# A residual chain with adapter feed-forward in three-pass products: where the adapters' small products stand among the large ones

## The chip, the cores and the metric

One NeuronCore of a Trainium2 chip runs one program. The metric is device microseconds of one launch. Three runs of the kernel before gave a median of 1245.07 us (1245.03 to 1245.76).

The engines are named as the profile names them: PE (TensorE, with PEld for its weight loads), DVE (VectorE), ACT (ScalarE), POOL (GpSimd) and SP (SyncE, which only issues transfers here).

## The reference, cut to what matters

Each of the 64 samples carries a 64 x 512 array `x`. Three small layers with weights gathered by sample come first, then a feed-forward layer with low-rank adapters, and each is added to `x`:

```python
x = x + einsum('bct,bcd->bdt', x, w0[subject])
x = x + einsum('bct,bcd->bdt', x, w1[adapter])
x = x + einsum('bct,bcd->bdt', x, w2[adapter]) + bias[adapter][:, :, None]

def lora_linear(x, W, A, B, idx):         # A: (8, in, 16), B: (8, 16, out)
    base = einsum('bsd,df->bsf', x, W)
    lora = einsum('bsr,brf->bsf', einsum('bsd,bdr->bsr', x, A[idx]), B[idx])
    return base + lora

gate = lora_linear(x, Wg, Ag, Bg, idx)    # 512 -> 2048
up = lora_linear(x, Wu, Au, Bu, idx)
x = x + lora_linear(silu(gate) * up, Wd, Ad, Bd, idx)   # 2048 -> 512
```

## The kernel before, in words

The samples are done in four quarters of 16 samples, each quarter as two token tiles t = 0 and 1 of 512 columns. The hidden dimension of 2048 is done in 16 blocks of 128; a unit b = -1 ahead of them, in quarters 1 to 3, makes the rank-16 inputs of the adapters. Every large product is made of three passes in fp32r (high by high, high by low part, low by high), so an operand needs a high part, made by an ACT copy, and a low part, made by a subtraction on DVE or POOL.

Gate and up of both token tiles are four products by a scheme of Strassen's kind with seven products (`A11, S1, S2, A12, S3, S4, A22`), each six matmuls of 512 columns (`product`, recorded at L1692). They stand in the PE's program in this order, in the banks px, py, px, pz, px, py, px. Between them come four groups of the **adapters' output products** (`lora`, L1709), three small matmuls each of 192, 256 and 192 columns that add to the bank of a result: lora11 (pz), lora21 (py), lora22 (pz), lora12 (px).

DVE takes the results out of the banks: **c11** (L1513, reads pz after lora11), **u3** (L1518, px after S3), **c12** (L1523, py after lora21), **c22** (L1570, pz after lora22), with `silu0` on ACT behind c11. Then **gate0** (L1565) and **gate1** (L1575) multiply gate and up. The result h is split into a high part (ACT copy, L915) and a low part (`h_low`, POOL, L769), which the down products need.

The **down phases** take h of two blocks ("half" 0 and 1) and one token tile. At the end of an odd block stands the phase for t = 0, which needs the h of that same block in its half 1, at the end of an even block the phase for t = 1 of the two blocks before. A block 15 has both. In each half there are four large products into the banks pd0 to pd3 (three matmuls each, L1692) and one **adapters' down product** into pv: four matmuls of 256 columns (`adapters_down`, L1736 and L1738). The order of the five is `order(d)`, j = 4 being the adapters' product. DVE adds the finished banks to `acc` and `vacc` (L1475, L1472). The adapters' down product needs the tile `ad`, whose low part POOL makes (`ad_low`, L769, tile ad) in each odd block; in POOL's program it stands behind a wait for **c11** of that block. In blocks 13 and 15 of quarters 0 to 2 POOL gathers rows for the next quarter (`gather_own`, L733) between ad_low and h_low.

Each engine runs its own program in written order. Semaphores tie them: a count such as `p2_mm` (lora11 done) or `c11_done` is raised by one instruction and waited for by others. In blocks 3 to 10 of quarters 0 to 2 the PE also makes the layers of the next quarter: a product at L1998 behind S2 and a fp32 product at L2031 behind S3 ("layer blocks"), with DVE and ACT steps of their own.

Of the kernel before, what the change touches and what calls it, by code (L numbers as in the profile page):

```python
# [11 lines left out]
ACT = mybir.ActivationFunctionType  # L12
# [78 lines left out]
def cond_resid_kernel(nc, x, subject, adapter, w0_rows, w1_pairs, w2_rows, bias_pairs, w_gu, w_dn, a_in_rows, ad_rows, b_rows, bd_rows, out):  # L91
# [6 lines left out]
    with ExitStack() as ctx:  # L98
# [216 lines left out]
        p6_mm = sem("p6_mm")  # L315
        p2_mm = sem("p2_mm")
        p7_mm = sem("p7_mm")
        p3_mm = sem("p3_mm")
# [48 lines left out]
        def made(q, i):  # L367

            return q * QP + i + 1

        def order(d):

            return (4, 0, 1, 2, 3) if stays(d) else (0, 1, 4, 2, 3)

# [159 lines left out]
        def _(sp):  # L534
# [104 lines left out]
            for q, b in units():  # L639
# [56 lines left out]
                if b == BLOCKS - 1 and q + 1 < QUARTERS:  # L696
                    for half in range(2):
                        sp.wait_ge(xops_out[half], TP * (q + 1) * 64)

                    for done, k in ((p1_mm, A11), (p5_mm, S1), (p2_mm, A12), (p4_mm, A22), (p6_mm, S2), (p7_mm, S3),  # L700
                                    (p3_mm, S4)):
                        sp.wait_ge(done, k_done)
                        for g, xo in enumerate((xo_hi, xo_lo)):
                            sp.dma_start(raw(xo[:, k, :]), xops[g, k]).then_inc(xop_in[k], 16)
                    load_down(blocks_done(q, b))
                    load_down(blocks_done(q, b) + 1)
                elif k is None and n and n + 2 < QUARTERS * UNITS:
                    next_weights(n)
# [204 lines left out]
        def _(act):  # L913
# [122 lines left out]
            for q, b in units():  # L1036
# [97 lines left out]
                if b != 1 and n > 1:  # L1134
                    act.wait_ge(p2_mm, k)
                    if split:
                        weights_high(n + 1, 1)
                act.wait_ge(c11_done, k)
                act.activation(g0[:, :], g0[:, :], ACT.Silu).then_inc(silu0_done, 1)
                if (q, b) == (0, BLOCKS - 1):  # L1140
                    own_selectors(1).then_inc(sel_done, 1)
                if n == 1:
                    weights_high(n + 1, 0)
                i = pair_at(q, b)
                if i is not None:
                    pair = PAIR_ORDER[i]
                    act.wait_ge(layer_mm, made(q, i))
                    add_bias(acc[:, (q + 1) % 2, pair, :], pd[0][:, :], (q + 1) * QP + pair).then_inc(layer_add, 1)

                def keep_c21():  # L1150
# [18 lines left out]
                if b == 1:  # L1169
                    act.wait_ge(p2_mm, k)  # L1170
                    weights_high(n + 1, 0)
                    weights_high(n + 1, 1)
# [34 lines left out]
        def _(dve):  # L1207
# [346 lines left out]
            for q, b in units():  # L1554
# [30 lines left out]
                if b == 0:  # L1585
                    if q:
                        v_low(q - 1, 1)
                        sums(n + 1)
                    c11(k)
                    if q:  # L1590
                        weights_low(n + 1, 0)
                    u3(k)
                    select(q, 1)
                    c12(k)
                    if not q:
# [42 lines left out]
                if to_own:  # L1638
                    own_difference(q + 1)
                c11(k)  # L1640

                behind = parts_at(q, b) is not None
# [6 lines left out]
                if behind:  # L1649
                    weights_low(n + 1, 1)  # L1650
                    token_low(q, parts_at(q, b))
                c12(k)
                gate0()
                if late:
                    sums(n + 1)
                    weights_low(n + 1, 0)
# [31 lines left out]
        def _(pe):  # L1688
# [97 lines left out]
            def down(q, m, t, layer=0, turned=0, finished=0):  # L1786

                d = phase(q, m, t)
                for half in range(2):
                    pe.wait_ge(h_lo_done[t], q * BLOCKS + 2 * m + half + 1)  # L1790
                    pe.wait_ge(dn_done, q * BLOCKS + 2 * m + half + 1)
                    for r, j in enumerate(order(d)):
                        if half == 0 and d:
# [8 lines left out]
                        if j == 4:  # L1802
                            if half == 0:
                                pe.wait_ge(ad_done, q * SUPER + m + 1)
                            ins = adapters_down(t, half)
                        else:
                            ins = split_product(pd[j][:, :], [s[:, j * P:(j + 1) * P] for s in hs],
# [139 lines left out]
            for q, b in units():  # L1947
# [6 lines left out]
                if b == -1:  # L1954
                    pe.wait_ge(c21_kept, k)
                    own_products(q, 1)
                    finish(q - 1, 0)
                    pe.wait_ge(c22_done, k)
                    select(q, 0)
                    continue  # L1960
# [46 lines left out]
                if fresh:  # L2007
                    tokens_ready(q, A12)
                product(pz, A12, True, True)

# [4 lines left out]

                if n > 1:
                    lora11()

                pe.wait_ge(w_done[2], n + 1)
# [3 lines left out]
                product(px, S3, False, True).then_inc(p7_mm, 1)  # L2023
                if n == 1:

                    lora11()
                if i is not None:
# [13 lines left out]
                if fresh:  # L2041
                    tokens_ready(q, S4)
                product(py, S4, False, True)
                lora(py, b, 1, 0).then_inc(p3_mm, 1)

# [5 lines left out]

                if b:
                    lora22()

                pe.wait_ge(w_done[3], n + 1)
# [3 lines left out]
                product(px, A22, False, True)  # L2059
                if b == 0:  # L2060
                    pe.wait_ge(b_got_in[1], (q * SUPER + 1) * CHUNKS * 16)
                    pe.wait_ge(u_done, 6 * q + 6)
# [98 lines left out]
```

## Time and profile before

| | before |
|---|---|
| median of 3 runs | 1245.07 us |
| span of the profiled execution | 1244.1 us |
| PE busy | 1235.7 us, 99% |
| PEld busy | 1036.6 us, 83% |
| DVE busy | 954.8 us, 77% |
| POOL busy | 713.4 us, 57% |
| ACT busy | 551.6 us, 44% |
| granted PE clock | 0.999 |

The page gives the span of the profiled execution, not a launch time of its own for it, so the span stands for it. A busy PE isn't a PE at its peak, since matmuls are pipelined: what a matmul costs is the distance from its start to the start of the next, which the timeline gives. A timeline row with x3 holds three instructions that touch, from the first one's start.

### The profile page before, as it was taken

What the parts mean: (1) busy time and instruction counts of PE and PEld (TensorE: products, weight loads), DVE (VectorE), ACT (ScalarE), POOL (GpSimd) and SP (SyncE); (2) the same over time, 40 slices, a digit from 0 to 9 for tenths busy, and PEclk for the clock granted to TensorE, in tenths of its full rate; (3) what the DMA queues carried; (4) which work ended last, traced back from release to release, by engine and by line L of the source; (5) the groups of instructions that cost most, each with busy time, mean ns of one, the idle gap of its engine ahead of it and who ended that gap; (6) DMA issues with size and microseconds to landing.
All of it is one profiled execution on the core that took longest, in us unless ns stands there. A gap on an engine that the chain in (4) does not pass through costs nothing.

```text
span 1244.1 us, 17944 instructions
## 1 busy us (share of the span) xinstructions
PE 1235.7 (99%) x6222; PEld 1036.6 (83%) x6222; DVE 954.8 (77%) x1531; ACT 551.6 (44%) x987; POOL 713.4 (57%) x598
## 2 busy tenths in 40 slices
PE   8999999999999999999999999999999999999998
PEld 7888888888888888888888888888888888888887
DVE  6987778887778777788778768777868877777775
ACT  3744454444434354554334444544534443444332
POOL 3576556558745556546865556564675554444553
PEclk9999999999999999999999999999999999999999
DMA  5866455544896345456398534545559742333433
GB/s 195 271 227 209 118 143 150 155 137 136 304 330 216 106 126 150 128 141 176 109 383 294 168 108 145 153 126 148 147 177 374 254 114 78 97 85 102 111 90 121
DMA packets 142199, 211.68 MB, mean 170 GB/s; under 512 B 44192, under 2 KB 88480, under 8 KB 142112
## 3 DMA queue, kind: packets, MB, share of 16 engines
q1 hardware_dynamic: 117696, 135.45, 34.5%
q0 software_dynamic: 23552, 73.95, 19.6%
q8 instruction: 51, 0.84, 0.3%
q10 hardware_dynamic: 864, 1.15, 0.3%
q14 instruction: 36, 0.29, 0.1%
HBM read 166.46 MB, written 44.04 MB: 169 GB/s over the span
## 4 chain that ended last, share of the span: by engine, by line
PE 96%; DVE 2%; DMA 0%; issue 0%; another core or an unknown queue 0%; DVEq 0%
PE px L1692 28%; PE pd L1692 28%; PE py L1692 14%; PE pz L1692 7%; PE pz L1709 3%; PE pv L1738 2%; PE pv L1736 2%; PE pd L2031 2%; PE py L1709 2%; PE px L1709 2%; PE pd L1861 1%; PE pd L1719 1%; PE py L1843 1%; PE px L1843 1%; PE pd L1828 1%; PE pd L1901 0%
## 5 line engine op out<-in xcount | busy, mean ns | idle before, releaser
L769 POOL TENSOR_TENSOR h_lo<-g,h_hi 128x512 fp32r<-128x512 f32 x127 | 182.9, 1440 | 283.6 <-ACT h_hi L915 281.3
L733 POOL DMA_INDIRECT b_got<-b_table,idx_b x192 | 199.4, 1039 | 58.0 <-issue 51.1
L1692 PE MATMUL px<-xo_hi,wg_hi 128*128 128x512 f32 x516 | 206.9, 401 | 1.1 <-DVE wg_lo L1345 0.8
L1475 DVE TENSOR_TENSOR acc<-pd,acc 128x512 f32<-128x512 f32 x248 | 164.7, 685 | 53.8 <-PE pd L1692 51.3
L1345 DVE TENSOR_TENSOR wg_lo<-w_raw,wg_hi 128x512 fp32r<-128x512 f32 (+1 forms) x256 | 182.3, 717 | 29.9 <-issue 17.9
L1692 PE MATMUL px<-xo_hi,wg_lo 128*128 128x512 f32 x516 | 202.4, 392 | 0.0
L1692 PE MATMUL px<-xo_lo,wg_hi 128*128 128x512 f32 x516 | 200.9, 389 | 0.0
L915 ACT ACTIVATE wg_hi<-w_raw 128x512 fp32r<-128x512 f32 (+1 forms) x260 | 146.0, 570 | 122.8 <-PE py L1709 77.0
L1692 PE MATMUL pd<-wd_hi,h_hi 128*128 128x512 f32 x504 | 199.7, 396 | 0.0
L1692 PE MATMUL pd<-wd_lo,h_hi 128*128 128x512 f32 x504 | 197.9, 393 | 0.0
L1692 PE MATMUL pd<-wd_hi,h_lo 128*128 128x512 f32 x504 | 196.6, 390 | 0.0
L915 ACT ACTIVATE h_hi<-g 128x512 fp32r<-128x512 f32 x128 | 80.9, 632 | 194.5 <-DVE g L1565 75.4
L1692 PEld LDWEIGHTS px<-xo_hi,wg_lo 128*128 128x128 f32 x516 | 96.8, 188 | 22.1
L1692 PEld LDWEIGHTS pd<-wd_hi,h_lo 128*128 128x128 f32 x504 | 94.6, 188 | 21.7
L1692 PE MATMUL py<-xo_hi,wg_hi 128*128 128x512 f32 x260 | 111.6, 429 | 0.0
L1692 PEld LDWEIGHTS px<-xo_hi,wg_hi 128*128 128x128 f32 x516 | 96.9, 188 | 17.4 <-DVE wg_lo L1345 1.0
L1692 PEld LDWEIGHTS px<-xo_lo,wg_hi 128*128 128x128 f32 x516 | 97.5, 189 | 15.6
L1692 PEld LDWEIGHTS pd<-wd_hi,h_hi 128*128 128x128 f32 x504 | 94.5, 188 | 13.9
L1692 PEld LDWEIGHTS pd<-wd_lo,h_hi 128*128 128x128 f32 x504 | 94.8, 188 | 12.9
L915 ACT ACTIVATE g<-px 128x512 f32<-128x512 f32 x64 | 38.4, 600 | 149.5 <-PE px L1692 138.9
L1575 DVE TENSOR_TENSOR g<-g,up 128x512 f32<-128x512 f32 x64 | 100.6, 1572 | 3.5 <-ACT g L1154 2.7
L1692 PE MATMUL py<-xo_hi,wg_lo 128*128 128x512 f32 x260 | 101.8, 391 | 0.0
(325 smaller groups left out, 2454.0 us busy)
## 6 DMA issues: line engine op xcount, KB each, us to landing
w_raw<-w_gu SPq DMA_DIRECT2D x65, 512.0 KB
wd_raw<-w_dn SPq DMA_DIRECT2D x64, 256.0 KB
xo_hi<-xops SPq DMA_DIRECT2D x21, 512.0 KB, 6.0
xo_lo<-xops SPq DMA_DIRECT2D x21, 512.0 KB, 7.3
acc<-x SPq DMA_DIRECT2D x8, 1024.0 KB, 8.7
ad_raw<-ad_table SPq DMA_DIRECT2D x16, 512.0 KB
xops<-st_hi SPq DMA_DIRECT2D x24, 256.0 KB, 2.7
xops<-st_lo SPq DMA_DIRECT2D x24, 256.0 KB, 2.9
```

The source lines that it names most:

```text
L733: gp.indirect_dma_start(out=dst, out_offset=None, in_=rows_of, in_offset=bass.IndirectOffsetOnAxis(ap=rows.bitcast(U32), axis=0)).then_inc ...
L769: return gp.tensor_tensor(dst, src_raw, src_hi, ALU.subtract)
L915: return act.activation(dst, src, ACT.Copy)
L1345: dve.tensor_tensor(wg_lo[:, lo:hi, :], src, wg_hi[:, lo:hi, :], ALU.subtract).then_inc(w_done[g], 1)
L1475: ins = dve.tensor_tensor(dst, pd[j][:, :], dst, ALU.add)
L1575: dve.tensor_tensor(g1[:, :], g1[:, :], up1[:, :], ALU.mult).then_inc(h_done[1], 1)
L1692: ins = pe.matmul(psum, w_parts[wi], x_parts[xi], start=(start and i == 0), stop=(stop and i == 2), skip_group_check=more)
L1709: ins = pe.matmul(psum[:, tokens], b_got[:, CHUNKS * t + c, first:first + P], u[:, m, t, cols], start=(start and c == 0), stop=True, skip_ ...
L1736: pe.matmul(pv[:, tok], ad[:, half, 2 * t + a, :, :].rearrange("p g n -> p (g n)"), hs[0][:, tok], start=(half == 0 and a == 0), stop=True ...
L1738: ins = pe.matmul(pv[0:HC, tok], ad[:, half, 2 * t + a, 0, :], hs[1][:, tok], start=False, stop=True, skip_group_check=True)
L1843: ins = pe.matmul(ua_bank(q, t, 0)[:, a * HALF:(a + 1) * HALF], w_parts[wi][:, cols], (xo_hi, xo_lo)[xi][:, k, tok], start=(cp == c == a = ...
L2031: pe.matmul(pd[0][:, :], f_one[:, :], acc[:, (q + 1) % 2, PAIR_ORDER[i], :], start=True, stop=True).then_inc(layer_mm, 1)
```

## The change

Four things move, and the number of instructions with work in them stays the same.

1. lora11 moves from behind A12 to behind S4, right ahead of lora21. A new count `a12_mm` tells the end of A12 to those who waited for it by `p2_mm`.
2. lora22 moves from behind lora21 to behind A22, right ahead of lora12 (blocks 1 to 15).
3. In the phases for t = 0, and in the last one of a quarter's t = 1, the adapters' down product is the first of half 0 and the last of half 1. In the other phases for t = 1 (`early`) the adapters' products of both halves are the first two of the phase. The last two phases of the program stay as they are.
4. DVE's and ACT's programs follow: c11 goes behind the low part of the weights and u3, silu0 behind it, `token_low` behind gate0.

```diff
+        def early(d):
+
+            return d % 2 == 1 and d % (2 * SUPER) != 2 * SUPER - 1
+
         def order(d):
 
-            return (4, 0, 1, 2, 3) if stays(d) else (0, 1, 4, 2, 3)
+            return (4, 0, 1, 2, 3) if stays(d) or early(d) else (0, 1, 2, 3, 4)
...
-                product(pz, A12, True, True)
+                product(pz, A12, True, True).then_inc(a12_mm, 1)
...
-                if n > 1:
-                    lora11()
...
                 product(py, S4, False, True)
+                lora11()
                 lora(py, b, 1, 0).then_inc(p3_mm, 1)
...
-                if b:
-                    lora22()
...
                 product(px, A22, False, True)
-                if b == 0:
+                if b:
+                    lora22()
+                else:
...
-                    for r, j in enumerate(order(d)):
+                    for r, j in enumerate(order(d) if half else (4, 0, 1, 2, 3)):
+                        if half and j == 4 and early(d):
+                            continue
...
                             ins = adapters_down(t, half)
+                            if half == 0 and early(d):
+                                pe.wait_ge(h_lo_done[t], q * BLOCKS + 2 * m + 2)
+                                adapters_down(t, 1).then_inc(down_mm, 1)
...
-                c11(k)
-
                 behind = parts_at(q, b) is not None
                 if not last and not behind and not late and not to_own:
                     weights_low(n + 1, 1)
...
                 if behind:
                     weights_low(n + 1, 1)
-                    token_low(q, parts_at(q, b))
+                c11(k)
                 c12(k)
                 gate0()
+                if behind:
+                    token_low(q, parts_at(q, b))
```

The last two pieces of the diff are DVE's, in blocks 1 to 15. In block 15 of quarters 0 to 2 the four weight sums of the next unit (`sums(n + 2)`) stand behind u3 as before, and so now ahead of c11. A wait for the last add into pv is new ahead of `select(q, 0)` in the unit b = -1. POOL's program isn't changed.

On the PE, in quarter 3 before: lora11 (pz<-u,b_got) between A12 (pz) and S3 (px).

```order
L1692 MATMUL pz<-xo_hi,wg_lo 128x512
L1709 MATMUL pz<-u,b_got 128x192
L1709 MATMUL pz<-u,b_got 128x256
L1709 MATMUL pz<-u,b_got 128x192
L1692 MATMUL px<-xo_hi,wg_hi 128x512
L1692 MATMUL px<-xo_lo,wg_hi 128x512
```

After, in the same quarter: behind S4 (py), with lora21, ahead of A22 (px).

```order
L1697 MATMUL py<-xo_hi,wg_lo 128x512
L1714 MATMUL pz<-u,b_got 128x192
L1714 MATMUL pz<-u,b_got 128x256
L1714 MATMUL pz<-u,b_got 128x192
L1714 MATMUL py<-u,b_got 128x192
L1714 MATMUL py<-u,b_got 128x256
L1714 MATMUL py<-u,b_got 128x192
L1697 MATMUL px<-xo_hi,wg_hi 128x512
```

Nothing small stands between A12 and the end of S4 any more; there are two places with six small matmuls a block in place of one with six and two with three.

The PE at the start of a phase of quarter 3 before, from the last matmul of lora12 (px<-u) on: pd0, pd1, then the adapters' product (pv<-h,ad).

```order
L1709 MATMUL px<-u,b_got 128x192
L1692 MATMUL pd0<-wd_hi,h_hi 128x512
L1692 MATMUL pd0<-wd_lo,h_hi 128x512
L1692 MATMUL pd0<-wd_hi,h_lo 128x512
L1692 MATMUL pd1<-wd_hi,h_hi 128x512
L1692 MATMUL pd1<-wd_lo,h_hi 128x512
L1692 MATMUL pd1<-wd_hi,h_lo 128x512
L1736 MATMUL pv<-h_hi,ad 128x256
L1738 MATMUL pv<-h_lo,ad 64x256
L1736 MATMUL pv<-h_hi,ad 128x256
L1738 MATMUL pv<-h_lo,ad 64x256
L1692 MATMUL pd2<-wd_hi,h_hi 128x512
```

After, the phase for t = 0: the adapters' product stands right behind lora12.

```order
L1714 MATMUL px<-u,b_got 128x192
L1741 MATMUL pv<-h_hi,ad 128x256
L1743 MATMUL pv<-h_lo,ad 64x256
L1741 MATMUL pv<-h_hi,ad 128x256
L1743 MATMUL pv<-h_lo,ad 64x256
L1697 MATMUL pd0<-wd_hi,h_hi 128x512
L1697 MATMUL pd0<-wd_lo,h_hi 128x512
L1697 MATMUL pd0<-wd_hi,h_lo 128x512
```

It needs `ad` six large matmuls earlier than before, and the other adapters' product of this phase has gone to its end.

DVE in a block of quarter 3 before: c11 is g0<-pz,g0, u3 is up1<-px,up1, c12 is up0<-py,up0, gate0 is g0<-g0,up0.

```order
L1345 TENSOR_TENSOR wg_lo<-w_raw,wg_hi 128x512
L1513 TENSOR_TENSOR g0<-pz,g0 128x512
L1345 TENSOR_TENSOR wg_lo<-w_raw,wg_hi 128x512
L1518 TENSOR_TENSOR up1<-px,up1 128x512
L1523 TENSOR_TENSOR up0<-py,up0 128x512
L1565 TENSOR_TENSOR g0<-g0,up0 128x512
L1570 TENSOR_TENSOR up1<-pz,up1 128x512
L1345 TENSOR_TENSOR wg_lo<-w_raw,wg_hi 128x512
L1575 TENSOR_TENSOR g1<-g1,up1 128x512
```

After, the same steps.

```order
L1350 TENSOR_TENSOR wg_lo<-w_raw,wg_hi 128x512 x2
L1523 TENSOR_TENSOR up1<-px,up1 128x512
L1518 TENSOR_TENSOR g0<-pz,g0 128x512
L1528 TENSOR_TENSOR up0<-py,up0 128x512
L1570 TENSOR_TENSOR g0<-g0,up0 128x512
L1575 TENSOR_TENSOR up1<-pz,up1 128x512
L1350 TENSOR_TENSOR wg_lo<-w_raw,wg_hi 128x512
L1580 TENSOR_TENSOR g1<-g1,up1 128x512
```

c11 now stands directly ahead of c12 and gate0.

## Rows read from the trace of the kernel before

**Rows 1.** The page, part 4: shares of the chain that ended last, by engine

```profile
PE 96%; DVE 2%; DMA 0%; issue 0%; another core or an unknown queue 0%; DVEq 0%
```

**Rows 2.** Timeline, PE, blocks 8 and 9 of quarter 3: start us, us, engine, line, operation

```profile
1099.67 0.48 PE L1709 MATMUL py<-u,b_got 128*128 128x192 f32 x3
1099.99 0.50 PE L1709 MATMUL pz<-u,b_got 128*128 128x192 f32 x3
1100.33 0.41 PE L1692 MATMUL px<-xo_hi,wg_hi 128*128 128x512 f32 x1
...
1101.74 0.48 PE L1709 MATMUL px<-u,b_got 128*128 128x192 f32 x3
...
1103.47 0.28 PE L1736 MATMUL pv<-h_hi,ad 128*128 128x256 f32 x1
...
1103.93 0.40 PE L1692 MATMUL pd<-wd_hi,h_hi 128*128 128x512 f32 x1
...
1107.14 0.40 PE L1692 MATMUL pd<-wd_hi,h_hi 128*128 128x512 f32 x1
...
1109.90 0.39 PE L1692 MATMUL py<-xo_hi,wg_hi 128*128 128x512 f32 x1
...
1113.98 0.48 PE L1709 MATMUL pz<-u,b_got 128*128 128x192 f32 x3
...
1117.09 0.48 PE L1709 MATMUL py<-u,b_got 128*128 128x192 f32 x3
```

**Rows 3.** Timeline, PE and PEld, the last block of the program

```profile
1221.57 0.48 PE L1709 MATMUL py<-u,b_got 128*128 128x192 f32 x3
...
1223.86 0.19 PEld L1736 LDWEIGHTS pv<-h_hi,ad 128*128 128x128 f32 x1
1223.95 0.30 PE L1736 MATMUL pv<-h_hi,ad 128*128 128x256 f32 x1
...
1224.44 0.40 PE L1692 MATMUL pd<-wd_hi,h_hi 128*128 128x512 f32 x1
...
1227.18 0.28 PE L1736 MATMUL pv<-h_hi,ad 128*128 128x256 f32 x1
```

**Rows 4.** Timeline, DVE and POOL, block 9 of quarter 3

```profile
1114.50 0.69 DVE L1513 TENSOR_TENSOR g<-pz,g 128x512 f32<-128x512 f32 x1 [1.14 <-PE pz L1709]
1115.27 1.74 POOL L769 TENSOR_TENSOR ad<-ad_raw,ad 128x512 fp32r<-128x512 f32 x1 [4.37 <-DVE g L1513]
...
1118.40 0.69 DVE L1565 TENSOR_TENSOR g<-g,up 128x512 f32<-128x512 f32 x1
...
1119.84 1.61 POOL L769 TENSOR_TENSOR h_lo<-g,h_hi 128x512 fp32r<-128x512 f32 x1 [2.83 <-ACT h_hi L915]
1120.30 1.69 DVE L1575 TENSOR_TENSOR g<-g,up 128x512 f32<-128x512 f32 x1
```

**Rows 5.** Tile ad on POOL (ns min/median/max), then timeline of block 1, quarter 1

```profile
L769 POOL TENSOR_TENSOR ad<-ad_raw,ad x32: 1278/1716/1746, 67.4 to 1219.8; 128x512 fp32r<-128x512 f32 x32
369.36 1.31 POOL L769 TENSOR_TENSOR ad<-ad_raw,ad 128x512 fp32r<-128x512 f32 x1
369.94 0.69 DVE L1518 TENSOR_TENSOR up<-px,up 128x512 f32<-128x512 f32 x1 [0.71 <-PE px L1692]
```

**Rows 6.** Timeline, DVE and PEld, block 2 of quarter 0

```profile
84.95 0.69 DVE L1518 TENSOR_TENSOR up<-px,up 128x512 f32<-128x512 f32 x1
...
85.76 0.19 PEld L1692 LDWEIGHTS px<-xo_hi,wg_hi 128*128 128x128 f32 x1 [0.51 <-issue]
```

**Rows 7.** Timeline, POOL, block 13 of quarter 1

```profile
592.67 0.96 POOL L733 DMA_INDIRECT st_lo<-a_in_rows,idx_own  x1
593.94 0.95 POOL L733 DMA_INDIRECT st_lo<-a_in_rows,idx_own  x1 [0.30 <-issue]
```

**Rows 8.** Timeline, DVE, block 15 of quarter 1

```profile
626.25 0.69 DVE L1518 TENSOR_TENSOR up<-px,up 128x512 f32<-128x512 f32 x1 [0.72 <-PE px L1692]
...
628.32 0.68 DVE L1523 TENSOR_TENSOR up<-py,up 128x512 f32<-128x512 f32 x1
```

More of the change, by code:

```diff
@@ L316, in cond_resid_kernel @@
         p2_mm = sem("p2_mm")
+        a12_mm = sem("a12_mm")
         p7_mm = sem("p7_mm")
@@ L698, in _ @@
                         sp.wait_ge(xops_out[half], TP * (q + 1) * 64)
-                    for done, k in ((p1_mm, A11), (p5_mm, S1), (p2_mm, A12), (p4_mm, A22), (p6_mm, S2), (p7_mm, S3),
+                    for done, k in ((p1_mm, A11), (p5_mm, S1), (a12_mm, A12), (p4_mm, A22), (p6_mm, S2), (p7_mm, S3),
                                     (p3_mm, S4)):
@@ L1134, in _ @@
                 if b != 1 and n > 1:
-                    act.wait_ge(p2_mm, k)
+                    act.wait_ge(a12_mm, k)
                     if split:
                         weights_high(n + 1, 1)
[L1138 to L1143, printed above, removed]
                 i = pair_at(q, b)
@@ L1148, in _ @@
                     add_bias(acc[:, (q + 1) % 2, pair, :], pd[0][:, :], (q + 1) * QP + pair).then_inc(layer_add, 1)
+                if (q, b) == (0, BLOCKS - 1):
+                    own_selectors(1).then_inc(sel_done, 1)
+                act.wait_ge(c11_done, k)
+                act.activation(g0[:, :], g0[:, :], ACT.Silu).then_inc(silu0_done, 1)
+                if n == 1:
+                    weights_high(n + 1, 0)
                 def keep_c21():
@@ L1169, in _ @@
                 if b == 1:
-                    act.wait_ge(p2_mm, k)
+                    act.wait_ge(a12_mm, k)
                     weights_high(n + 1, 0)
@@ L1639, in _ @@
                     own_difference(q + 1)
-                c11(k)
                 behind = parts_at(q, b) is not None
@@ L1650, in _ @@
                     weights_low(n + 1, 1)
-                    token_low(q, parts_at(q, b))
+                c11(k)
                 c12(k)
                 gate0()
+                if behind:
+                    token_low(q, parts_at(q, b))
                 if late:
@@ L1958, in _ @@
                     pe.wait_ge(c22_done, k)
+                    pe.wait_ge(down_add, added(phase(q - 1, SUPER - 1, 1), 4))
                     select(q, 0)
@@ L2023, in _ @@
                 product(px, S3, False, True).then_inc(p7_mm, 1)
-                if n == 1:
-                    lora11()
                 if i is not None:
```

## The prediction

> **What bounds the kernel now.** I read the chain of waits first: 96% of it is the PE itself, and DVE has 2% [rows 1]. So time can only come from the distances between the PE's matmuls, or go into waits of the PE that aren't there yet. Then I read the PE's timeline for distances from start to start. Eighteen large matmuls far from any small one take 1113.98 - 1109.90 = 4.08 us, 0.227 us each. The six of A22, right behind adapters' products, take 1101.74 - 1100.33 = 1.41 us, not 1.36. A group of three small ones takes 0.32 us (1099.67 to 1099.99), and 0.34 us when it follows another group (to 1100.33). So a small group costs its own time and slows what comes behind, for some ten matmuls: the twelve behind an adapters' down product take 1109.90 - 1107.14 = 2.76 us, not 2.72 [rows 2]. Last I read DVE and POOL around c11, ad_low and gate0 [rows 4, 5], since the change moves c11.
>
> **What the PE gains.** From one lora21 to the next a plain block (no layer product) takes 1117.09 - 1099.67 = 17.42 us before [rows 2]. After, from the same rows: lora11 and lora21 0.32 + 0.34; A22 1.41; lora22 and lora12 0.32 + 0.34; then the down phase. An adapters' product behind lora stands once in the trace: 1224.44 - 1223.95 = 0.49 us, and twelve large ones behind it take 2.74 us to 1227.18 [rows 3]. Elsewhere the product takes 1103.93 - 1103.47 = 0.46 us [rows 2].
> - Phase t = 0: 0.49 + 24 large ones (2.74 + 2.72) + 0.46, then twelve at 2.76 and 24 undisturbed ones at 5.44. With the 2.73 us of the groups and A22 that is 17.34 us, 0.08 less.
> - Phase t = 1, both products first: 0.49 + 0.47 + 5.46, then 36 undisturbed at 8.16: 17.31 us, 0.11 less.
>
> In the 24 layer blocks the layer product still stands before S4, and moving lora11 saves nothing: of its 0.04 to 0.05 us the second group's 0.02 and the slow matmuls behind the layer product eat all. They keep 0.03 and 0.06. Of the 28 t = 0 blocks (1 to 13) 16 are plain, and likewise of the 28 with t = 1 (2 to 14): 16 x 0.08 + 12 x 0.03 + 16 x 0.11 + 12 x 0.06 = 4.1 us. Blocks 0 and 15, worked the same way, add about 0.5. The gain is **4.6 us**. Merging two groups itself gains nothing (0.34 against 0.32); it is the undisturbed S3 and S4 and the undisturbed 24 down products that gain.
>
> **What the new places wait for.** I count from M, the end of lora21 (1221.57 + 0.48 = 1222.05 in the last block). The PE wants the weights `ad` at 1223.86, M + 1.81, when the adapters' product is right behind lora12 [rows 3]. Before, it stood six large ones (1.41 us) later, and ad_low began at c11's end three to four us before M: 1115.19 to 1115.27 [rows 4]. Now lora11 ends 0.34 before M. c11 starts 0.04 behind lora11's end (1114.46 to 1114.50), takes 0.69, and POOL starts 0.08 behind it: M + 0.47 [rows 2, 4]. How long does ad_low take there? Its median is 1.72 us, but 1.31 when only a DVE step that reads a bank runs beside it, u3 here [rows 5]. The 1.74 of block 9 has the low part of the weights, both inputs in SBUF, running at its start. In its new place it begins beside c12, which reads a bank, and gate0 comes later. I take 1.30: the end is at M + 1.77. From a releaser's end to the PE's next weight load took 85.76 - 85.64 = 0.12 us [rows 6]. So the weights come at M + 1.89, **0.07 to 0.08 us late** in 28 odd blocks: 2.1 us; bounds 0 (0.1 us of luck in the chain) and 0.5 us a block (ad_low at its median).
>
> The Trainium skill, SBUF — State Buffer, section "Who interferes with whom", says that a DVE instruction with at most one SBUF input doesn't contend with GpSimd, that one with two does, and that issue order decides who is blocked. By that rule ad_low keeps 1.30 and gate0 waits for it. The trace agrees for u3 (1.31 beside 0.69) [rows 5].
>
> **Gate0 is held.** gate1, begun under h_low, ended 1121.99 - 1121.45 = 0.54 us behind it [rows 4]. gate0 would start at M + 1.18 and end 0.54 behind ad_low, at M + 2.31, against M + 1.52 before. The h_high copy and the hand-over take 1119.84 - 1119.09 = 0.75 us [rows 4], and h_low 1.61 with the weights' low part at its start: M + 4.67, ready for a weight load at M + 4.79. The PE wants it at half 1, M + 1.90 + 0.49 + 2.74 - 0.23 = M + 4.90 [rows 3], and 0.07 later with the wait above. It is covered, with 0.2 us left.
>
> Block 13 of quarters 0 to 2 isn't. Between ad_low and h_low POOL issues two gathers, the last of which ends 594.89 - 592.53 = 2.36 us behind ad_low [rows 7]: M + 4.13. h_low takes 1.3 to 1.6 and ends at M + 5.4 to 5.7, while the PE can go without a wait up to M + 4.85. That is 0.5 to 0.8, say 0.65 us, three times: **1.9 us** (0 if the gathers shift earlier).
>
> Block 15 of quarters 0 to 2: the four sums behind u3 take 628.32 - 626.25 = 2.07 us with u3 [rows 8]. u3 starts at M - 2.01 (S4 and two groups, 2.05, ahead of M, plus 0.04), so c11 starts at M + 0.06 instead of M - 0.30, and `ad` is 0.37 later still: 0.45 us, three times, **1.4 us** (bounds 0.9 and 1.8).
>
> Unit b = -1: the last add into vacc is now the fifth, not the third, so the fold and mask behind it come later and with them the low part that the first product of block 0 waits for; I take 0.15 us, three times, 0.4 us, bounded by 0 and by two adds, 1.3 us each. The last block and the start (block 2 of quarter 0 waits for u3 today) 0.2 us. The new wait ahead of `select` is hidden by the products in front of it. The wait of lora22 for c11 is hidden by A22: c11 ends at M + 0.39, the weights are wanted at M + 1.1. The later c11 delays `silu0` and `token_low`, whose users come a block later; SP's stores and the load of ad_raw behind them move with them and have several us.
>
> **Sum.** -4.6 + 2.1 + 1.9 + 1.4 + 0.4 + 0.2 = +1.4 us. The span of the profiled execution is 1244.1 and the median 1245.07, 0.97 above; I keep that distance: 1244.1 + 1.4 + 0.97 = **1246.5 us**.
>
> **Rivals.**
> - *The waits stay away.* If ad_low or its hand-over is 0.08 us shorter than I build it, and the gathers of block 13 don't push h_low, only 0.9 to 1.5 us of waits is left: -3.4 us, 1241.7. For it: 0.07 us is within the roundings of a chain of five rows. Against it: blocks 13 and 15 don't hang on roundings. 21%.
> - *The new waits grow (slower).* One mechanism, ad_low in the odd blocks: each 0.1 us that it ends later costs 2.8 us over 28 blocks. The result turns slower from 0.03 us a block with the rest as it is, and is over 0.2% from 0.12. If it takes its median of 1.72 in the new place, the wait is 0.5 us: 12 us more, 1258; halfway, 1252. For it: 24 of 32 ad_low stand near 1.72. Against it: those have another step beside them. 22%.
> - *No gain at the seams.* The slow matmuls behind small ones might belong to what they read and stay, so that only the waits come: 1245.07 + 6.0 = 1251. Against it: the same 1.41 stands behind every lora group. 6%. The Trainium skill, TensorE: Matmul & The Clock Gate, section "Back-to-back issue gap", gives one distance for each width, whatever stands before (512 columns: 216 ns by its formula). By that rule no order of matmuls gains. The trace has 227 ns undisturbed and 235 on average in A22, so it differs.
> - *My sum*, 51%: 1243.5 to 1248.5.
>
> **How the numbers follow.** What a measurement can tell from no change is about 0.2%, 2.5 us: below 1242.6 is faster, above 1247.6 slower. Faster has the first rival, 0.20, and a sliver of my own case, 0.01. Slower has the second, the third and 0.10 of my own case: 0.38. Within it 0.41. The range leaves out the tail of the second rival and half of the first: 1241.8 to 1250.6.
>
> **What would show it.** In the new trace S3 and S4 without anything small between take 2.72 us; 24 down products stand in a row at 5.46; ad_low starts 0.47 behind lora21's end and lasts 1.30; gate0 lasts over 1.0 us in odd blocks; the first weight load of the adapters' down product starts 1.88 behind lora21's end instead of 1.81, and in blocks 13 and 15 of the first three quarters the PE stands for half a microsecond. The prediction is wrong if ad_low lasts 1.7 there, if blocks 13 have no wait, or if A22's 1.41 us turns up in S3 as well.

## The result

| | before | after |
|---|---|---|
| median | 1245.23 us (4 runs) | 1263.24 us (1258.95 to 1265.07, 4 runs) |
| span of the profiled execution | 1244.1 | 1257.1 |
| PE busy | 1235.7 | 1237.0 |
| DVE busy | 954.8 | 979.1 |
| chain that ended last: PE, DVE | 96%, 2% | 89%, 6% |

The ratio is 1.0138 (1.0127 to 1.0150): 18 us slower by the medians, where 1.4 us were forecast and the range ended at 1250.6. The profiled execution (1258.95 us) is the fastest of the four, 13.0 us longer in span than before. The median is 4.3 us above it, and the other three executions have no profile. The chain's shares answer to [rows 1]:

```profile
PE 89%; DVE 6%; issue 1%; DMA 1%; POOL 1%; ACT 1%; DVEq 0%; ACTq 0%
```

**Where the blocks are as forecast.** The PE's and POOL's timelines of block 9, quarter 3, after, answer to [rows 2, 4]; then the tile ad on POOL, as in [rows 5]:

```profile
1127.08 0.39 PE L1697 MATMUL px<-xo_hi,wg_hi 128*128 128x512 f32 x1
...
1129.80 0.48 PE L1714 MATMUL pz<-u,b_got 128*128 128x192 f32 x3
1130.12 0.50 PE L1714 MATMUL py<-u,b_got 128*128 128x192 f32 x3
...
1132.54 0.36 PE L1741 MATMUL pv<-h_hi,ad 128*128 128x256 f32 x1
...
1133.08 0.40 PE L1697 MATMUL pd<-wd_hi,h_hi 128*128 128x512 f32 x1
...
1138.54 0.28 PE L1741 MATMUL pv<-h_hi,ad 128*128 128x256 f32 x1
```
```profile
1130.32 0.69 DVE L1518 TENSOR_TENSOR g<-pz,g 128x512 f32<-128x512 f32 x1 [0.99 <-PE pz L1714]
1131.71 1.22 DVE L1570 TENSOR_TENSOR g<-g,up 128x512 f32<-128x512 f32 x1
```
```profile
1131.09 1.30 POOL L774 TENSOR_TENSOR ad<-ad_raw,ad 128x512 fp32r<-128x512 f32 x1 [7.07 <-DVE g L1518]
```
```profile
L774 POOL TENSOR_TENSOR ad<-ad_raw,ad x32: 1280/1296/1304, 65.9 to 1235.3; 128x512 fp32r<-128x512 f32 x32
```

S3 and S4, twelve large products, take 1129.80 - 1127.08 = 2.72 us, and the 24 down products 1138.54 - 1133.08 = 5.46. lora21 ends at 1130.62; this end is M, as in the prediction. ad_low starts at M + 0.47 in 29 of the 32 odd blocks (M + 0.85 in the three blocks 15 of quarters 0 to 2) and takes 1.30 in all 32; the weights for pv are taken in at M + 1.88 in the blocks 1 to 13 (2.26 in those three blocks 15); gate0 is held and takes 1.22 in place of 0.69. All of that stood in the forecast.

**Where the time is.** From the view of the PE's waits, after (engine, tile and line, what was waited for, us in all, times, longest); before, every wait in this view lies in the program's start and its first blocks:

```profile
PE pv L1741 <- DVE vacc L1477: 3.5, 3, 1.4
PE py L1853 <- DVE wg_lo L1345: 2.5, 3, 1.5
...
PE px L1697 <- ACT up L920: 1.5, 4, 0.4
PE py L1853 <- issue: 1.4, 2, 1.1
PE pd L1697 <- POOL h_lo L774: 1.2, 3, 0.4
...
PE px L1697 <- DVE up L1523: 1.0, 1, 1.0
PE pv L1741 <- POOL ad L774: 0.7, 3, 0.2
PE px L1697 <- issue: 0.5, 1, 0.5
```

L1853 is the adapters' first products of the next quarter (`own_products`), which stand between the two phases of block 15. To place the loss I took, from the PE's timeline, the distance from the end of one lora21 to the end of the next (us; the three numbers are the ends of quarters 0, 1 and 2):

| | block 15 to block 0 of the next quarter | block 13 to 14 | 14 to 15 (with a phase t = 1) | 9 to 10, quarter 3 (with a phase t = 0) |
|---|---|---|---|---|
| before | 34.21, 34.21, 34.22 | 17.41, 17.41, 17.41 | 17.41 | 17.41 |
| after | 37.15, 38.41, 38.63 | 18.82, 18.83, 18.83 | 17.33 | 17.40 |

The three quarter ends cost 2.94 + 4.20 + 4.42 = 11.6 us and the three blocks 13 cost 1.41 + 1.42 + 1.42 = 4.2. The rest is -2.8 us: -2.8 up to the first lora21 (50.8 us from the PE's first step, 53.6 before; over all profiles of this study 50.8 to 54.3, so one span alone tells nothing below some 3 us), +1.2 in the next three blocks, +0.2 at the end of the program, and -1.4 in all the others. Without the shorter start the span would have grown by 15.8 us.

**The quarter end, before.** ACT's, DVE's, POOL's and PE's timelines at the end of quarter 1, where lora21 of block 15 ends at M = 627.91:

```profile
633.01 1.14 ACT L915 ACTIVATE wg_hi<-st_lo 128x512 fp32r<-128x512 f32 x2
```
```profile
633.66 1.29 DVE L1340 TENSOR_TENSOR wg_lo<-st_lo,wg_hi 128x512 fp32r<-128x512 f32 x2 [1.22 <-ACT wg_hi L915]
```
```profile
627.06 1.05 POOL L733 DMA_INDIRECT st_lo<-a_in_rows,idx_own  x1
```
```profile
636.28 0.28 PE L1843 MATMUL py<-xo_hi,wg_hi 128*128 128x256 f32 x1
```

**And after**, where M = 631.60 (ACT, DVE, POOL, PE):

```profile
640.08 1.15 ACT L920 ACTIVATE wg_hi<-st_lo 128x512 fp32r<-128x512 f32 x2 [2.42 <-DMA st_lo<-a_in_rows,idx_own]
```
```profile
640.74 2.73 DVE L1345 TENSOR_TENSOR wg_lo<-st_lo,wg_hi 128x512 fp32r<-128x512 f32 x2 [3.75 <-issue]
643.39 2.47 DVE L1480 TENSOR_TENSOR acc<-pd,acc 128x512 f32<-128x512 f32 x4
645.79 0.67 DVE L1477 TENSOR_TENSOR vacc<-pv,vacc 128x512 f32<-128x512 f32 x1
```
```profile
632.45 1.28 POOL L774 TENSOR_TENSOR ad<-ad_raw,ad 128x512 fp32r<-128x512 f32 x1 [3.60 <-DVE g L1518]
633.88 1.24 POOL L738 DMA_INDIRECT st_lo<-a_in_rows,idx_own  x1
```
```profile
640.25 0.28 PE L1743 MATMUL pv<-h_lo,ad 128*64 128x256 f32 x1
641.58 0.35 PE L1853 MATMUL py<-xo_hi,wg_hi 128*128 128x256 f32 x1 [1.05 <-issue]
...
643.62 0.36 PE L1853 MATMUL py<-xo_hi,wg_hi 128*128 128x256 f32 x1 [0.38 <-issue]
...
646.72 0.35 PE L1741 MATMUL pv<-h_hi,ad 128*128 128x256 f32 x1 [1.44 <-DVE vacc L1477]
```

Read it from POOL down. The last gather of the next quarter's weights is behind ad_low and so behind c11. It was issued at M - 0.85 and is now issued at M + 2.28. Before, ACT's copy of it began 5.95 us behind the issue, right behind another copy; now it begins 6.20 behind the issue and waited 2.42 for the transfer. DVE's low part is late by it, and the first `own_products` start at M + 9.98, where the row of matmuls would have had them at M + 8.77 (0.12 us behind the start of 640.25). The second low part runs beside POOL's h_low and is longer, and `own_products` wait a second time (643.62). In DVE's program the five adds of the phase stand behind the low parts, the add out of pv as the last, and the next phase begins with pv: 1.44 us more. That is three waits in a row, with one late transfer at the head of them. (At the end of quarter 0 the low parts take their 1.29 us: 0.8 and 0.6 us of waits and, in block 0, the 0.5 of the last line of the waits.)

### The profile page after: what moved, and what is told of

The parts are those of the page before. It is cut to its first block, busy times and chain, and to the rows that moved or that the text cites. A ratio compares the mean times of both kernels' runs of the same rounds, so it can differ in the third digit from the quotient of the medians.

```text
span 1257.1 us, 17947 instructions
## 1 busy us (share of the span) xinstructions
PE 1237.0 (98%) x6222; PEld 1037.6 (83%) x6222; DVE 979.1 (78%) x1531; ACT 542.4 (43%) x987; POOL 709.9 (56%) x598
## 4 chain that ended last, share of the span: by engine, by line
PE 89%; DVE 6%; issue 1%; DMA 1%; POOL 1%; ACT 1%; DVEq 0%; ACTq 0%
PE px L1697 27%; PE pd L1697 25%; PE py L1697 13%; PE pz L1697 6%; PE pz L1714 3%; PE pv L1741 2%; PE pv L1743 2%; PE pd L2036 2%; PE px L1714 2%; PE py L1714 1%; PE pd L1871 1%; DMA st_lo<-a_in_rows,idx_own 1%; PE pd L1724 1%; DVE acc L1480 1%; PE px L1853 1%
## 5 line engine op out<-in xcount | busy, mean ns | idle before, releaser
L774 POOL TENSOR_TENSOR h_lo<-g,h_hi 128x512 fp32r<-128x512 f32 x127 | 180.3, 1420 | 232.9 <-ACT h_hi L920 231.7
L1350 DVE TENSOR_TENSOR wg_lo<-w_raw,wg_hi 128x512 fp32r<-128x512 f32 (+1 forms) x256 | 196.6, 775 | 74.9 <-ACT wg_hi L920 52.7
L1697 PE MATMUL pd<-wd_hi,h_hi 128*128 128x512 f32 x504 | 196.9, 391 | 1.2 <-POOL h_lo L774 1.2
L774 POOL TENSOR_TENSOR ad<-ad_raw,ad 128x512 fp32r<-128x512 f32 x32 | 41.5, 1296 | 166.5 <-DVE g L1518 166.5
L1151 ACT ACTIVATE g<-g 128x512 f32<-128x512 f32 x64 | 40.5, 632 | 173.8 <-DVE g L1518 173.8
L1580 DVE TENSOR_TENSOR g<-g,up 128x512 f32<-128x512 f32 x64 | 107.3, 1676 | 3.1 <-ACT g L1159 2.8
```

The source lines that it names most:

```text
L774: return gp.tensor_tensor(dst, src_raw, src_hi, ALU.subtract)
L1350: dve.tensor_tensor(wg_lo[:, lo:hi, :], src, wg_hi[:, lo:hi, :], ALU.subtract).then_inc(w_done[g], 1)
L1580: dve.tensor_tensor(g1[:, :], g1[:, :], up1[:, :], ALU.mult).then_inc(h_done[1], 1)
L1697: ins = pe.matmul(psum, w_parts[wi], x_parts[xi], start=(start and i == 0), stop=(stop and i == 2), skip_group_check=more)
```

## The experiments

The ratio is to runs of before on the same chip; the last two columns are the distances of the table above, from the profiled execution.

| kernel | median us | before us | ratio (95%) | quarter ends | blocks 13 to 14 |
|---|---|---|---|---|---|
| 1, gate part only | 1257.1 | 1245.6 | 1.0091 (1.0071 to 1.0110) | 39.37, 35.46, 35.37 | 18.13, 18.85, 18.10 |
| 2, down order only | 1243.03 | 1245.6 | 0.9977 (0.9965 to 0.9988) | 34.23, 34.65, 34.27 | 17.38 (all) |
| 3, after, gathers moved | 1247.29 | 1245.6 | 1.0009 (0.9999 to 1.0019) | 34.99, 34.97, 35.22 | 17.43, 17.40, 17.40 |
| 4, after, old order in block 15 | 1262.24 | 1245.6 | 1.0126 (1.0099 to 1.0153) | 37.89, 37.25, 39.58 | 18.83, 18.77, 18.77 |
| 5, as 3, ad_low early | 1246.35 | 1243.16 | 1.0026 (1.0017 to 1.0035) | 35.71, 35.75, 36.00 | 17.34 (all) |
| 6, before, POOL late | 1250.99 | 1243.16 | 1.0065 (1.0049 to 1.0080) | 34.65, 35.01, 34.98 | 17.77 (all) |
| 7, as 5, c11 ahead of sums | 1244.22 | 1243.16 | 1.0009 (1.0000 to 1.0018) | 35.11, 35.10, 35.38 | 17.34 (all) |
| 8, as 5, sums behind gate0 | 1242.69 | 1243.79 | 0.9992 (0.9983 to 1.0001) | 34.74, 34.77, 34.15 | 17.34 (all) |
| 9, as 2, again | 1241.39 | 1243.79 | 0.9983 (0.9973 to 0.9992) | 34.10 (all) | 17.38 (all) |
| 10, after, h_low of t = 1 early | 1260.35 (1 run) | 1245.66 | | 39.35, 35.82, 39.55 | 18.10, 18.15, 18.11 |

**1, the gate part alone.** The kernel after, with the down phases of before:

```diff
-            return (4, 0, 1, 2, 3) if stays(d) or early(d) else (0, 1, 2, 3, 4)
+            return (4, 0, 1, 2, 3) if stays(d) else (0, 1, 4, 2, 3)
```

> The kernel after, with the down phases as they were before: only lora11 and lora22, DVE's and ACT's order are changed. Theory T (late gather): POOL waits for c11 ahead of ad_low in every odd block, and c11 now comes three to four us later, so the two gathers of block 13 push h_low back and the gather of block 15 lands late. The loss of blocks 13 and 14 (1.4 us, three times) and the wait of the next quarter's first weights (1.4 us, three times) stay, the wait for the add into pv goes: 1250 to 1256 us, about 1253. Rival R (bank order): the loss at the quarter's end comes from pv being the last of one phase and the first of the next; then it is gone here, and only blocks 13 and 14 are left: 1246 to 1248.

It took 1257.1, a little over theory T's range and far from rival R's. The first `own_products` for quarter 1 waited longer than in the kernel after, with no add out of pv ahead of the low part (PE's timeline):

```profile
336.57 0.35 PE L1844 MATMUL py<-xo_hi,wg_hi 128*128 128x256 f32 x1 [3.47 <-DVE wg_lo L1341]
```

So the larger part of the loss, 11.5 us of 18, comes with the part of the change that moves c11. At the other two ends the copy began at M + 7.66 and M + 6.91 and 1.2 us each were lost.

**2, the order of the down products alone,** in the kernel before (the phases' pieces of the diff ahead and nothing of the gate's).

> The kernel before, with only the order of the adapters' down products changed, pv first of half 0 and last of half 1, both first in early phases. c11 and POOL stand as before. Theory T: POOL's gathers are in time, so the add into pv isn't late either; what is left is the gain of longer runs of large matmuls, some 2 us: 1242 to 1245, about 1243. Rival R: the quarter ends lose 3 us each as in the kernel after: 1251 to 1256.

1243.03, as T has it: faster than before. Each plain block takes 0.03 to 0.04 us less, and two of the three quarter ends lose nothing, with pv last in one phase and first in the next. So the order by itself is no cause while the transfer is in time. The third end, 34.65, lost 0.44: there ACT waited for the transfer though it was issued as early as before, and the first product of block 0 waits (ACT, then PE):

```profile
632.65 1.15 ACT L919 ACTIVATE wg_hi<-st_lo 128x512 fp32r<-128x512 f32 x2 [0.38 <-DMA st_lo<-a_in_rows,idx_own]
```
```profile
651.22 0.47 PE L1696 MATMUL px<-xo_hi,wg_hi 128*128 128x512 f32 x1 [0.34 <-issue]
```

A copy that starts 0.47 us later than before costs nearly all of it here: the row of DVE steps from that low part to block 0 has no room with this order.

The two parts don't add up: alone they are 11.5 us slower and 2.6 us faster, together 18.0 slower. Some 6 us of the rest are waits that only both together have in the profiles: for the add out of pv (3.5 us), and for ad, 0.06 us in 28 blocks and some 0.4 in three blocks 15. The others aren't placed.

**3, the gathers moved** in the kernel after (POOL's program):

```diff
+                if to_own and b % 2:
+                    gather_own(q + 1, range(11, 12) if b == BLOCKS - 3 else range(7, 8))
                 if b % 2:
                     gp.wait_ge(c11_done, k)
                     ad_low(q, b // 2)
...
-                if to_own:
-                    gather_own(q + 1, {-3: range(11, 13), -2: (), -1: range(7, 8)}[b - BLOCKS])
...
                     h_low(q, b, 0)
+                if to_own and b == BLOCKS - 3:
+                    gather_own(q + 1, range(12, 13))
```

> The kernel after, with three gathers of each of the first three quarters moved in POOL's program: in block 13 one of the two stands ahead of the wait for c11 and ad_low, the other behind h_low, in block 15 the one stands ahead of the wait for c11. Theory T: the losses of blocks 13 and 14 (4.2 us) and nearly all of the quarter ends (11.6 us, of which some 0.5 each stays as the wait for ad) go, and with them the spread of the runs: 1243 to 1248, about 1246. Rival R: only blocks 13 and 14 come back, 4 us: 1257 to 1260.

1247.29: 16 us of the 18 come back from the place of three instructions in each quarter, and the loss of blocks 13 to 14 is gone. That is T's, and R is out. Of the PE's waits these two lie behind the first blocks, the second being that for ad in the blocks 15:

```profile
PE px L1699 <- issue: 0.9, 3, 0.5
PE pv L1743 <- POOL ad L774: 0.7, 3, 0.2
```

**4, the old order in the two phases of block 15.**

```diff
+            if d % (2 * SUPER) >= 2 * SUPER - 2 and not stays(d):
+                return (0, 1, 4, 2, 3)
```

> The kernel after, with the two phases of block 15 of the first three quarters in the order of before (pv third in both halves). Theory T: the gather of block 15 is as late as before this edit, so the first weights of the next quarter are still waited for; only the wait for the add into pv (1.44 us in the profile) and the wait for ad (0.4 us) go, three times each: 4 to 6 us less than the kernel after, 1257 to 1260. Rival R: all of the loss at the quarter ends goes, 9 to 11 us: 1250 to 1254.

1262.24, by its ratio not told apart from the kernel after: less of a gain than T said, and nothing of R's. The wait for pv is gone, and the one for the weights is longer (the PE's and DVE's rows at the end of quarter 2):

```profile
953.84 0.36 PE L1855 MATMUL py<-xo_hi,wg_hi 128*128 128x256 f32 x1 [3.59 <-DVE wg_lo L1347]
```
```profile
951.40 2.89 DVE L1347 TENSOR_TENSOR wg_lo<-st_lo,wg_hi 128x512 fp32r<-128x512 f32 x2 [4.16 <-ACT wg_hi L922]
```
```profile
951.85 1.28 POOL L776 TENSOR_TENSOR h_lo<-g,h_hi 128x512 fp32r<-128x512 f32 x1
```

Here the transfer was 6.81 us from issue to ACT's copy. The two low parts then fall beside POOL's h_low and take 2.89 in place of 1.29 us. So with pv third in both phases its add isn't waited for, with the low parts this late. That the edit itself makes the transfer longer isn't shown: in experiments 1, 4 and 10, whose gather is issued at the same M + 2.28 to 2.30 as in the kernel after, the time from issue to copy lies between 4.60 and 7.20 us over nine quarter ends, and the ends with less than 5.4 us lose 1.2 to 1.6, the others 3 to 5.4. So one profile of such an end says little of its edit; the medians do.

**5, ad_low early** as well:

```diff
-                    gp.wait_ge(c11_done, k)
+                    gp.wait_ge(p7_mm, k)
                     ad_low(q, b // 2)
```

> The kernel after with the gathers moved as in the run on the gathers (1247.3 us), and ad_low of every odd block waiting for the end of S3 (p7_mm) instead of c11. Theory T: the adapters' down product waits 0.07 to 0.08 us for ad in the 28 odd blocks 1 to 13 and some 0.4 in three blocks 15 (with the restart of the row of matmuls 0.25 more there); all of it goes, since ad_low starts two microseconds before lora21's end: 2 to 3.5 us less, 1243.8 to 1245.3. gate0 is no longer held by ad_low: 0.69 us in place of 1.22. Rival R: the blocks with t = 0 do not get faster, because the 0.07 us is the restart behind lora and not a wait for ad; 1246.5 to 1247.5.

In the blocks T holds: the distance behind an odd block is 17.34 us, not 17.40, and gate0 is at 0.69. Each of the 28 blocks had waited 0.06 us. But the whole, 1.0026, is over T's range and no better than experiment 3's, since the three blocks 15 have a new wait (the PE's, DVE's and POOL's rows at the end of quarter 1):

```profile
632.01 0.49 PE L1716 MATMUL pz<-u,b_got 128*128 128x192 f32 x2 [1.17 <-DVE g L1520]
```
```profile
628.05 2.17 DVE L1336 TENSOR_TENSOR w_raw<-w_raw 128x256 f32<-128x256 f32 x1
630.15 0.41 DVE L1337 TENSOR_TENSOR w_raw<-w_raw 128x256 f32<-128x256 f32 x1
...
631.27 0.68 DVE L1520 TENSOR_TENSOR g<-pz,g 128x512 f32<-128x512 f32 x1
```
```profile
628.64 1.30 POOL L774 TENSOR_TENSOR ad<-ad_raw,ad 128x512 fp32r<-128x512 f32 x1
```

The first of the four weight sums takes 2.17 us, where the next takes 0.41, and ends 0.28 behind ad_low, which ran beside it; in [rows 8] all four sums and u3 take 2.07. c11 stands behind the sums and lora22 waits for it. Neither theory had this.

**6, only POOL late, in the kernel before:**

```diff
-                    gp.wait_ge(c11_done, k)
+                    gp.wait_ge(p3_mm if to_own else c11_done, k)
                     ad_low(q, b // 2)
```

> The kernel before with one edit: in blocks 13 and 15 of the first three quarters POOL's ad_low waits for lora21 (p3_mm) instead of c11, so the gathers behind it are issued some three us later; PE's, DVE's and ACT's programs are those of before. Theory T: the late gather alone brings the loss: the next quarter's first weights are 0.5 to 4 us late at each of the three quarter ends, and h_low of block 13 up to 0.5 us: 1247 to 1256, about 1250, with a spread between runs of several us. Rival R: POOL's lateness alone is covered and the loss needs the new order on DVE and PE as well: 1245 to 1246.

1250.99, 1.0065: T's. PE, DVE and ACT have their programs of before, and POOL's steps alone, with the gather issued at M + 1.79 instead of M - 0.85 (2.64 us later), cost 8 us in the median. So lateness on POOL is a cause by itself, of 8 of the 18 us. The profiled execution is the mildest of the four (span 1245.6, the others 1248.6 to 1249.7): its quarter ends lose 2.0 us and its blocks 13 1.1, and where the others lose more no profile shows. The PE's wait in it, then POOL's gather and ACT's copy at the end of quarter 1 (M = 627.53):

```profile
PE py L1843 <- DVE wg_lo L1340: 1.2, 3, 0.5
```
```profile
629.32 1.24 POOL L733 DMA_INDIRECT st_lo<-a_in_rows,idx_own  x1
```
```profile
635.10 1.15 ACT L915 ACTIVATE wg_hi<-st_lo 128x512 fp32r<-128x512 f32 x2 [1.99 <-DMA st_lo<-a_in_rows,idx_own]
```

**7 and 8, the sums of block 15.** Experiment 5 with `sums(n + 2)` between c11 and c12 (7), and behind gate0 (8):

```diff
-                if to_own:
-                    sums(n + 2)
                 if behind:
                     weights_low(n + 1, 1)
                 c11(k)
                 c12(k)
                 gate0()
+                if to_own:
+                    sums(n + 2)
```

> As the run with the gathers and ad_low moved, and in block 15 of the first three quarters c11 ahead of the four weight sums (sums) on DVE, not behind. Theory T: c11 and gate0 of block 15 come 0.4 us earlier, but with ad no longer waiting for c11 nothing on the PE waits for them, so at most 0.1 us a quarter: within 0.5 us of that run, 1243.5 to 1245.3. Rival R: the sums are wanted by the unit after (its weights), and behind c11 they come late: 1 to 3 us more than that run.

> As the run with gathers, ad_low and sums moved (1.0009 of before), with the four weight sums of block 15 behind gate0 instead of between c11 and c12. Theory T: in that run c12 ended at lora21's end + 2.53 us and h_low at + 5.42, and half 1 of the first phase waited 0.2 to 0.4 us for it at each of three quarter ends; now c12 ends at + 0.98, h_low is in time and 1.2 to 2 us go. Then all waits of the change are gone and only the gain of longer rows of large matmuls is left, less half a microsecond at the start: 0.9980 of before, range 0.9970 to 0.9995. Rival R: the sums now come late for the unit behind, which waits: 1.001 or more.

7 is at 1.0009, 8 at 0.9992 (0.9983 to 1.0001). In 7 the wait of lora22 is gone, and c12 and h_low are late instead (35.1 to 35.4 us at the ends). 7 is 2.1 us faster than 5, where T gave at most 0.1 us a quarter and R a loss: T had left out the wait of lora22 for c11. 8 takes that away too. It still loses 0.5 us at two of the three ends and 0.6 in the first blocks, and is level with before or a little better, where T hoped for 0.9980.

> The kernel with only the order of the adapters' down products changed, a second time, beside the run above on the same chip. It had 0.9977 of before (0.9965 to 0.9988) and its profile shows 0.03 to 0.04 us less in each block, 1.9 us in all. Theory T: 0.9975 to 0.9990 again. Rival R: the first ratio was luck in the spread of before's runs and it stands at 0.9995 to 1.0005.

0.9983 (0.9973 to 0.9992), beside 8 on the same chip. The version that beats both kernels is the smallest: before with the down order alone.

**10, the second wait behind block 13.** In the kernel after S3 of block 14 waits for ACT's copy of S2's bank (1.5 us in the waits above, with one of block 1). `h_low` of t = 1 in block 13 is put ahead of the last three gathers of the adapters' rows:

```diff
-                if b == BLOCKS - 1:
+                if b == BLOCKS - 1 or to_own and b == BLOCKS - 3:
                     h_low(q, b, 1)
...
-                if b < BLOCKS - 1:
+                if b < BLOCKS - 1 and not (to_own and b == BLOCKS - 3):
                     h_low(q, b, 1)
```

The two waits in the kernel after, block 13 of quarter 1 and S3 of block 14 (PE's timeline):

```profile
601.21 0.50 PE L1697 MATMUL pd<-wd_hi,h_hi 128*128 128x512 f32 x1 [0.39 <-POOL h_lo L774]
601.54 0.40 PE L1697 MATMUL pd<-wd_lo,h_hi 128*128 128x512 f32 x1
...
610.60 0.47 PE L1697 MATMUL px<-xo_hi,wg_hi 128*128 128x512 f32 x1 [0.44 <-ACT up L920]
```

> The kernel after, with POOL's h_low for t = 1 of block 13 in the first three quarters ahead of the last gathers of adapters' rows, some four us earlier than now. In the kernel after, S3 of block 14 waits 0.4 us in each of the three quarters: ACT copies S2's bank (up<-px) 1.05 us behind S2's end instead of 0.24, because the count of S2's end (p6_mm) rises 0.94 to 0.97 us behind the modelled end of its last matmul, while that h_low and DVE's low part of the weights, both begun 0.1 to 0.2 us before, run side by side. Theory T: the overlap brings it; with h_low elsewhere the stretch from block 13 to 14 takes 18.2 us in place of 18.8, and S3 of block 14 does not wait. Rival R: it has to do with the gathers' traffic or with the place in the program, and S3 of block 14 waits as before: 18.8. The whole is not told apart by one run: 1256 to 1264.

The distance went to 18.10 to 18.15 us, and S3 of block 14 did not wait in any of the three quarters. So of the 1.41 us of blocks 13 to 14, 0.70 is h_low of t = 0 behind the two gathers, and 0.71 this. That DVE's and POOL's steps side by side hold the copy isn't shown, and the record speaks against it as the whole cause: in experiment 1 the same h_low and low part run side by side in all three quarters and only the one with 18.85 has the wait, and in experiment 6 they do so in all three without it. So the cause of the 0.71 us stays open, and three quarters without the wait are a thin proof that moving h_low removed it.

## Why the prediction was wrong

- **The gain of the blocks.** Right in kind, a little large. 0.08 (t = 0) and 0.11 us (t = 1) were forecast for plain blocks; measured are 0.07 (17.41 to 17.34, without the wait for ad) and 0.08 (to 17.33). Layer blocks gained 0.02 and 0.04 for 0.03 and 0.06 (experiment 5 against before). Over the 56 blocks 1 to 14 that is 3.2 us for 4.1.
- **The wait for ad in 28 blocks.** Right: 0.06 us (17.40 against 17.34), ad_low at 1.30 from M + 0.47, gate0 held.
- **Block 13.** The mechanism was right, the size not: 0.65 us forecast, 1.41 measured. h_low is 0.4 late, as worked out, and the row of matmuls restarts at a longer distance (0.33 us from the first to the second); the other half is the wait of S3 in block 14, which no term of the sum has.
- **Block 15 and unit b = -1.** This is the step that failed. The prediction says that `ad` is 0.37 later there (right: 0.38), and prices block 15 at 0.45 us and the unit at 0.15, 1.8 us for the three ends; measured are 11.6. It followed POOL's gathers behind ad_low in block 13 and put the one of block 15 at nothing, without a reason. In the trace of before: issue at M - 0.85, copy by ACT at M + 5.10, products at M + 8.37. The gather moves by 3.13 us, and between the copy's start and the products there were 8.37 - 5.10 - 1.50 = 1.8 us of room (1.50 from the copy's start to the first product, 640.08 to 641.58). That alone gives 1.3 us at each of three ends; measured are 2.9 to 4.4, with the lengthened low parts, the add out of pv, the wait for ad and transfers of 5.94 to 6.60 us from issue to copy in the kernel after.
- **The add out of pv.** Forecast at 0.15 us, bounded by 1.3 us for two adds. It costs 0.6 to 1.4 us at each end, and needs two things together: all five adds stand behind the late low parts, and pv is the last of them and the first of the next phase. The bound counted the place in the order alone, and that costs next to nothing while the transfer is in time (experiment 2); with pv third and the low parts late (experiment 4) nothing waits for it. That block 0's first product hangs on this row, as the prediction says, showed at one end of experiment 2, with 0.34 us.
- **The start and the last block.** 0.2 us forecast, 1.4 measured. 0.6 lies in block 2 of quarter 0, where gate0, held by ad_low, lengthens a row of DVE steps that is late already: A22 waits 1.0 us for u3, 0.4 before; with ad_low early it is 0.5. Another 0.6 lies in block 0 of quarter 0, stays with ad_low early, and is there in experiment 1 and not in 2, so it comes with the gate's part. 0.2 lies at the end.
- **The rivals.** "The new waits grow" gave 1252 to 1258, near the profiled execution, but its mechanism, ad_low at 1.7 us, isn't there. "No gain at the seams" is wrong: the gain is there, 0.07 to 0.08 us a block.
- **The spread.** The first four runs of before lie within 0.7 us, the four of the kernel after within 6.1, eleven of experiment 9 within 1.7. That late transfers make this spread isn't shown: 17 runs of before on another chip lie within 5.0, the ten of experiment 3, whose gathers are early, within 3.5. The forecast had a distance of 0.97 us from span to median for both; after, the median is 6.1 above the profiled span. A launch is 1.8 to 2.2 us above the span of its own execution in all runs that have both, so the 0.97 compared two different executions.

## What to carry to other kernels

When a step of one engine moves, go through the program of every engine that waits for it, down to what is queued behind the waiting instruction, and write the new issue time of each transfer beside the time its data is wanted; a gather that is issued 3 us later is late by 3 us less the room that it had (here 1.3 us). A wait put in only to pace an engine (here POOL's for c11) carries all that stands behind it along. Of a change with several parts, run each alone: the smaller half was worth 2 to 3 us, and the other half cost 11 to 12. And run them together as well: the 18 us of both are more than the sum, since the order of one part makes a wait out of the lateness of the other.

## What the runs showed of the hardware that was not expected

- The same gather, issued at the same point of a block, was read between 4.60 and 7.20 us behind its issue (ACT waited for it each time), both ends of that range in one execution (experiment 1).
- A 256-column DVE step with all of it in SBUF took 2.17 us beside POOL's ad_low, and 0.42 alone, though by the rows it began 0.6 us ahead of ad_low and would have been done before it (experiment 5, all three quarters). Two low parts of 512 columns took 2.3 to 2.9 beside h_low and 1.29 alone. In these places ad_low and h_low kept their 1.27 to 1.31. POOL issued a gather until ad_low began; in before such an issue left the sums at 0.42 (end of quarter 1). Why the step that began first was held stays open.
- The count of S2's end (p6_mm) in block 14 rose 0.93 to 0.97 us behind the modelled end of its last matmul in the kernel after, while the next six matmuls went on at 0.227 us. Why stays open; with POOL's h_low elsewhere (experiment 10) it did not, and in experiment 1 it did in one quarter of three.
